# Other slots for the steps of a software pipeline, and other places for the pieces of the maxima

## The reference, cut to what matters

```python
x = x + layernorm(attn(layernorm(x)))     # first layer
x = x + layernorm(ffn(layernorm(x)))      # second layer

# attn: within one token; 16 heads of 16
Q, K, V = rms(x) @ Wq.T, ... ; pQ, pK = elu(Q), elu(K)
kv1 = sum over h of K1[h]^T V[h]; kv2 likewise with K2     # 8 x 16 each
a = Q1 @ kv1 - lmb * (Q2 @ kv2)           # per head
a = (1 - LAMBDA_INIT) * rms(a, g2); a = rms(a, g3) + a
out = gelu(a @ W1.T) @ W2.T + a

# ffn: causal attention with 16 query and 4 key heads of 16, rope,
# then a mixture of experts: 8 experts of width 512, the best 2 of each token
h = clip(x + softmax(mask(q k^T / 4)) v @ Wo)
out = clip(h + sum over the 2 experts of w * (silu(h Wg) * (h Wu)) Wd)
```

## Time and profile before

| | us |
|---|---|
| median of 3 runs | 3368.0 |
| lowest, highest | 3363.05, 3370.25 |
| the profiled execution | 3372.2 |
| its span (first to last instruction) | 3370.3 |
| mean granted clock of TensorE | 0.941 |

### The profile page before, as it was taken

One profiled execution on the slowest core, in us unless ns is written; L12 is line 12 of the kernel. 1 busy time (PEld: TensorE's weight loads), 2 busy tenths in 40 slices (PEclk: granted clock), 3 DMA queues, 4 the chain that ended last, 5 costly groups with the idle time before them and its releaser, 6 DMA issues. The chain is left out here.

```text
span 3370.3 us, 54068 instructions
## 1 busy us (share of the span) xinstructions
PE 2875.5 (85%) x17348; PEld 1707.3 (51%) x17349; DVE 2161.4 (64%) x4652; ACT 1670.3 (50%) x3836; POOL 1732.7 (51%) x2301
## 2 busy tenths in 40 slices
PE   4566899899989889989988998988759999999990
PEld 3344545554545554554555454443336666666650
DVE  3566887888898888888888888667322222222226
ACT  1234657667657656666765765765412222222224
POOL 5686746765765865776676575241212222222221
PEclk8788999999999999999999999999779999999995
DMA  1000000000000000000000000002243333333326
GB/s 46 0 10 10 11 9 14 14 25 12 27 22 14 28 20 17 22 19 23 17 22 27 12 24 19 12 25 81 73 112 53 57 58 57 58 52 58 58 43 200
DMA packets 102670, 123.21 MB, mean 37 GB/s; under 512 B 14384, under 2 KB 90160, under 8 KB 102448
## 3 DMA queue, kind: packets, MB, share of 16 engines
q1 hardware_dynamic: 76720, 85.54, 8.6%
q0 software_dynamic: 25728, 34.88, 6.0%
HBM read 58.23 MB, written 61.36 MB: 35 GB/s over the span
## 5 line engine op out<-in xcount | busy, mean ns | idle before, releaser
L822 ACT ACTIVATE wd<-SP_ 128x512 f32<-128x512 f32 (+3 forms) x1536 | 722.9, 488 | 477.9 <-PE SP_ L1439 334.0
L1105 DVE TENSOR_REDUCE NM<-MX 128x1 f32<-128x512 f32 (+3 forms) x1216 | 763.6, 655 | 243.9 <-PE MX L1396 145.2
L1393 PE MATMUL MX<-KST,QST 96*128 96x512 bf16 (+3 forms) x1536 | 457.5, 336 | 101.5 <-DVE NM L1105 89.2
L509 POOL TENSOR_TENSOR wg<-wu 128x1024 f32<-128x1024 f32 x256 | 487.4, 1924 | 106.3 <-DVE wu L941 106.2
L1436 PE MATMUL SP_<-QST,KST 99*128 99x512 bf16 (+3 forms) x1536 | 500.9, 333 | 34.3 <-ACT wd L822 15.8
L1718 POOL DMA_INDIRECT scratch_h<-Y,XG x136 | 211.2, 1553 | 604.5 <-DVE Y L1781 511.1
L1759 DVE TENSOR_TENSOR AG<-UB,SL 128x512 f32<-128x512 f32 x136 | 94.1, 692 | 460.3 <-PE UB L1798 456.9
L1736 ACT ACTIVATE SL<-GB 128x512 f32<-128x512 f32 x136 | 81.2, 597 | 603.4 <-PE GB L1798 603.4
L954 DVE TENSOR_TENSOR wg<-wu,SUM 128x1024 f32<-128x1024 f32 x256 | 310.4, 1213 | 99.7 <-PE SUM L1290 99.7
L1393 PEld LDWEIGHTS MX<-KST,QST 96*128 96x128 bf16 x1536 | 135.7, 98 | 433.9 <-DVE NM L1105 303.5
L1453 PE MATMUL OA<-wd,V 128*32 128x512 f32 (+3 forms) x3072 | 332.7, 506 | 1.0 <-ACT wd L822 0.4
(11 more groups left out here) (244 smaller groups left out, 4974.0 us busy)
## 6 DMA issues: line engine op xcount, KB each, us to landing
XG<-scratch_xs SPq DMA_DIRECT2D x136, 130.0 KB, 2.1
wu<-in_L_attn_x SPq DMA_DIRECT2D x64, 128.0 KB, 2.1
scratch_x<-wu SPq DMA_DIRECT2D x64, 128.0 KB, 1.7
scratch_h<-H SPq DMA_DIRECT2D x64, 128.0 KB, 1.7
X<-scratch_x SPq DMA_DIRECT2D x16, 512.0 KB, 4.0
HH<-scratch_h SPq DMA_DIRECT2D x16, 512.0 KB, 4.8
out<-X SPq DMA_DIRECT2D x16, 512.0 KB, 3.2
wg<-in_L_ffn_Wg SPq DMA_DIRECT2D x8, 512.0 KB
```

The lines of the kernel that those rows point to most:

```text
L509: sg["prod1"].by(pool.tensor_tensor(P1[:, k // 2, (k % 2) * hh * D:(k % 2 + 1) * hh * D].rearrange("p (h e d) -> p h e d", h=hh, e=HD), QK ...
L822: sg["exp"].by(act.activation(PR[:, n % 8, q0:512], SP_[:, n % 2, q0:512], ACT.Exp))
L1105: sg["mx"].by(dve.tensor_reduce(NM[:, u % 2, part, i, h:h + heads], MX[:, index % 2, 0:heads * n].rearrange("p (h n) -> p h n", n=n), AX.X ...
L1393: m = pe.matmul(out[:, k], QST[0:MROW, j % 2, g * G + h + k, i * P:(i + 1) * P], KST[0:MROW, keys % RK, g, 0:n], start=k == 0, stop=not la ...
```

## The change

No instruction is added or removed; steps get another slot, or another place within one. By engine:

- SP: the load of x tile p + 3 goes from slot 4 to slot 21 (tiles 0 to 2 are loaded ahead of the loop, as before); the h2 store from slot 14 (tile p - 17) to slot 0 of the next period (tile p - 18); the x1 store from slot 19 to 20.
- POOL: a period's order was `head_roots`, `gain2`, `row_root`, `copies`, `rotate`, `add_gains`, scatter 0, three `key_products`, scatter 1, `clip`, `flat_root`, `x_coefficients`, `out_coefficients`, the fourth `key_products`, scatter 2, `x1_coefficients`, scatter 3. Now it is `head_roots`, scatter 3 of the period before, `row_root`, `gain2`, `copies`, scatter 0, `rotate`, `add_gains`, three `key_products`, `clip`, `flat_root`, scatter 1, `x_coefficients`, `out_coefficients`, the fourth `key_products`, scatter 2, `x1_coefficients`.
- ACT: `squares(p - 1)` ahead of `first_part(p - 8)` in slot 2; `k_stacked` slot 12 to 14; `row_squares` slot 14 to 13; `squares2` slot 16 to 15.
- DVE: `query_products(p, 1)` from slot 7 to the head of slot 6; `add_attention` ahead of `flatten` in slot 18; `logits` slot 21 to 20.
- PE: `stack_keys` slot 12 to 13; `route` ahead of `transpose_attention` in slot 20.
- `LATE` and `AHEAD` of the maxima for rows with even j (index 0), and `share`, `LAST_BACK` and the scatters written in another way.

```diff
-        LATE, AHEAD, DONE, SPREAD = (2.5, 1.6), (9.2, 6.2), (2.0, 3.0), (3.5, 8.5)
+        LATE, AHEAD, DONE, SPREAD = (2.2, 1.6), (7.9, 6.2), (2.0, 3.0), (3.5, 8.5)
...
+        PHASE = 12 * SLOTS + 0
         LAST_PERIOD = TT + 24
-        LAST_BACK = TT + 12
+        LAST_BACK = START // SLOTS + TT
...
-            n = 32 if p % 8 < 4 else 16
-            return (i + 1) * n // SLOTS - i * n // SLOTS
+            k = p * SLOTS + i - PHASE
+            n = 16 if k < 0 or k // (NT // 2 * SLOTS) % 2 == 0 else 32
+            k %= SLOTS
+            return (k + 1) * n // SLOTS - k * n // SLOTS
...
+                        if i == 21 and have(p + 3):
+                            load(p + 3)
...
-                        if i == 4 and p >= 0 and have(p + 3):
-                            load(p + 3)
...
+                def spread(k, n):
+                    t = CH * (k // CH) + 2 * (k % CH) + n // 2
+                    scatter(t, n % 2)
...
-                        if i == 2 and have(p - 1):
+                        if i == 1 and have(p - 1):
                             head_roots(p - 1)
-                        if i == 4 and have(p - 1):
+                        if i == 2 and (p - 24) % CH < 2 and have(p - 24):
+                            spread(p - 24, 3)
+                        if i == 3 and have(p - 2):
+                            row_root(p - 2)
+                        if i == 6 and have(p - 1):
                             gain2(p - 1)
-                        if i == 4 and have(p - 2):
-                            row_root(p - 2)
...
-                        if i in (9, 12, 19, 21) and (p - 23) % CH < 2 and have(first):
-                            n = (9, 12, 19, 21).index(i)
-                            scatter(first + n // 2, n % 2)
...
                         if i == 6 and have(p):
+                            query_products(p, 1)
+                        if i == 6 and have(p):
                             query_sums(p, 0)
                         if i == 6 and have(p - 1):
                             norm_heads(p - 1)
-                        if i == 7 and have(p):
-                            query_products(p, 1)
...
+                        if i == 18 and have(p - 6):
+                            add_attention(p - 6)
                         if i == 18 and have(p - 17):
                             flatten(p - 17)
-                        if i == 18 and have(p - 6):
-                            add_attention(p - 6)
...
-                        if i == 21 and have(p - 18):
+                        if i == 20 and have(p - 18):
                             logits(p - 18)
```

More of the change, by code:

```diff
@@ L367, in load @@
                 def load(t):
+                    if t in first_loads:
+                        return
                     if t >= RX:
@@ L409, in _ @@
                     for i in range(SLOTS):
+                        if i == 0 and have(p - 18):
+                            t = p - 18
+                            need("h2", t + 1)
+                            sg["h2out%d" % (t % 2)].by(sp.dma_start(h2d[:, t, :], H2[:, t % 2]), 16)
+                        if i == 20 and have(p - 6):
+                            t = p - 6
+                            need("x1", t + 1)
+                            sp.dma_start(x1d[:, t, :], X[:, t % RX]).then_inc(stored[t % RX], 16)
+                        if i == 21 and have(p + 3):
+                            load(p + 3)
                         if p - TT in (8, 9, 10, 11) and i in (3, 15):
@@ L623, in _ @@
                             clip(p - 17)
+                        if i == 15 and (p - 23) % CH < 2 and have(p - 23):
+                            spread(p - 23, 1)
                         if i == 15 and have(p - 17):
@@ L631, in _ @@
                             key_products(p + 1, 3)
+                        if i == 20 and (p - 23) % CH < 2 and have(p - 23):
+                            spread(p - 23, 2)
                         if i == 20 and have(p - 6):
                             x1_coefficients(p - 6)
-                        first = CH * ((p - 23) // CH) + 2 * ((p - 23) % CH)
-                        if i in (9, 12, 19, 21) and (p - 23) % CH < 2 and have(first):
-                            n = (9, 12, 19, 21).index(i)
-                            scatter(first + n // 2, n % 2)
                 for r in range(2 * CH):
@@ L833, in _ @@
                             flat_turned(p - 18)
+                        if i == 2 and have(p - 1):
+                            squares(p - 1)
                         if i == 2 and have(p - 8):
                             first_part(p - 8)
-                        if i == 2 and have(p - 1):
-                            squares(p - 1)
                         if i == 2 and have(p - 7):
@@ L857, in _ @@
                             values(p + 1)
-                        if i == 12 and have(p - 8):
-                            k_stacked(p - 8)
                         if i == 13 and have(p - 17):
                             context_turned(p - 17)
-                        if i == 14 and have(p - 1):
+                        if i == 13 and have(p - 1):
                             row_squares(p - 1)
-                        if i == 16 and have(p - 17):
+                        if i == 14 and have(p - 8):
+                            k_stacked(p - 8)
+                        if i == 15 and have(p - 17):
                             squares2(p - 17)
@@ L1492, in _ @@
                             transpose_context(p - 17)
-                        if i == 12 and have(p - 8):
+                        if i == 13 and have(p - 8):
                             stack_keys(p - 8)
@@ L1502, in _ @@
                             stack_queries(p - 8, 1)
+                        if i == 20 and have(p - 18):
+                            route(p - 18)
                         if i == 20 and have(p - 2):
                             transpose_attention(p - 2)
-                        if i == 20 and have(p - 18):
-                            route(p - 18)
                         if i == 20 and have(p + 2):
```

6 lines of the change are left out of this document (5 added, 1 removed).

## The result

| | before | after |
|---|---|---|
| median | 3366.8 (5 runs) | 3381.9 (5 runs, 3378.7 to 3387.2) |
| ratio to before | | 1.0047, 95% interval 1.0032 to 1.0062 |
| profiled execution, its span | 3372.2, 3370.3 | 3380.5, 3378.6 |
| mean granted clock in that span | 0.941 | 0.937 |

The changed kernel is slower, by 15 us, where the forecast was 13 us faster. In its listing, lines from `attention()` on stand 15 further down (norm_heads L975 is L990, the maximum L1105 is L1120), POOL's 7. The page's part 1 answers the earlier trace rows: the same instructions, VectorE 3.5 and TensorE 3.8 us busier.

A forecast was written before the change was run, and what follows sets the result against it. TensorE and VectorE, both nearly full, take turns as the bound, coupled by MX's two buffers and SUM. -9 - 3 - 3 + 4 - 2 = -13 us gives 3359 profiled, 3355 as median; range 3336 to 3374.

The forecast's parts named there:

- Step 2: POOL: row_root ahead of gain2, scatter 3 behind head_roots; norm_heads keeps cover and its company on POOL: 0, bounds ±0.34 each.
- step 3: VectorE and TensorE: add_attention ahead of flatten, route ahead of transpose_attention; shortens nine long copies in routing steps: -3 us.
- Step 1: VectorE: query_products ahead of query_sums and norm_heads fills gaps before the products in long periods: -9 us, bounds -13.7 and 0.
- Steps 3 and 4: add_attention ahead of flatten, route ahead of transpose_attention, -3 us; logits to slot 20, removing TensorE's waits for it, -3 us.
- Step 5: New LATE and AHEAD: the first piece of an even row's maxima moves out of TensorE's free time: +4 us, bounds 0, +4.
- Steps 6 and 7: POOL's scatters and clip, ScalarE's moves, stack_keys, and SP's loads and stores: 0, save -2 us at the front's end.
- The tail's -2: POOL at the front's very end: one scatter moves behind clip, with add_attention's edit in the last periods: -2 us, bounds 0, -3.
- norm_heads is held up by rotate: Rival, VectorE beside POOL: each norm_heads in long and some light periods grows by 0.34 us: +6 to +8, 3362; chance 0.10.
- VectorE holds MX too long: Rival: three VectorE operations in a row without a maximum make TensorE wait: +11 to +18 us, 3379 at nearer end; chance 0.15.
- The likeliest case: The forecast itself, for the whole kernel: -13 us, to a median of 3355 us; chance 0.42.

The follow-up runs named there:

- a_old_pool_late: The changed kernel with POOL's order and LATE and AHEAD of the kernel before, other edits kept: 3359.8 us, ratio 0.9977 to the kernel before.
- b_34_products: The kernel before with query_products ahead of query_sums and norm_heads, add_attention ahead of flatten, route ahead of transpose_attention, logits in slot 20: 3358.3 us, ratio 0.9975.
- a_products_back: The changed kernel with query_products(p, 1) back behind query_sums and norm_heads on VectorE: 3374.6 us, ratio 1.0025 to the kernel before.

## Why the prediction was wrong

- **Step 2, the step that failed.** It named the case (norm_heads beside rotate), costed it at 0 and bounded it by the difference of two durations, 0.75 and 0.41 us: 0.34 in each. The runs show 1.6 to 2.1 us in each of ten hits, set by the length of the row (2.50 with four multiplications, 4.38 with eight), and TensorE's lower clock on top. The difference was misread: both durations had company already. In period 32 of the kernel before norm_heads starts 0.48 us into rotate's row and goes at once, and POOL gives way; in 33 it starts 0.54 us into it, not beside copies, and goes after the running instruction:

```profile
990.74 0.80 POOL L572 TENSOR_TENSOR RB<-Q,rope 128x160 f32<-128x160 f32 x1
...
1031.39 0.70 POOL L571 TENSOR_TENSOR RA<-Q,rope 128x160 f32<-128x160 f32 x1
```

38 of the 64 norm_heads start inside rotate's row in the kernel before, and none is held to its end; that it could be was not in the rows. A larger price was: the copy of 1.83 us, which stands still for a whole instruction of POOL, was used in step 3 and not here. The moves of scatters 0 and 3 weren't weighed for norm_heads beyond its wait for gain2, and they make the loss: with both back the time is 3354.7. For that wait the cover was read in p = 33 alone; in light periods such as 29 and 37 it was 0.1 us. The changed kernel shows no such wait, as costed, since norm_heads is later too.
- **Step 1** held: -9 forecast, -8.3 measured, and in p = 33 no gap stands between norm_heads and the next maximum. It shortens TensorE's waits for maxima by 11.5 us. VectorE in period 33 of the changed kernel answers the earlier trace rows:

```profile
1032.86 0.65 DVE L990 TENSOR_TENSOR wu<-wu,R 128x256 f32<-128x256 f32 x1
1033.42 1.14 DVE L1120 TENSOR_REDUCE NM<-MX 128x1 f32<-128x512 f32 x2
```

- **Steps 3 and 4**, -3 and -3: the waits changed as told. But five of the 16 copies were long (1.83 us), not nine; four took 0.40 to 0.62 and seven 0.16 or 0.17, so step 3 was too large from its own rows. The copy of 1.83 us is 1.57 now and TensorE's wait behind it 0.83 instead of 1.09, below; the sums of period 37 have no wait. The time did not follow.
- **Step 5**, +4: wrong in sign, -3 to -7. Perhaps the pieces that come one or two slots later help more than the first one costs; no run shows where the gain comes from.
- **Steps 6 and 7**, ScalarE, SP and `stack_keys` 0: right as far as can be told (a_old_pool_late less b_34_products is +1.5, within the intervals). The tail's -2 did not come: from the start of period 63 to that of the last `clip` both kernels take 393.8 us.
- **TensorE's clock** was not in the sum. It makes half of the difference in the long stretch.

```profile
1092.21 1.57 DVE L1073 CAST FX<-topi 128x4 f32<-128x4 uint32 x1
```

```profile
1095.85 1.97 PE L1296 MATMUL SUM<-ident,wg 128*128 128x128 f32 x16 [0.83 <-DVE BR L1098]
```

The rivals: "norm_heads is held up by rotate" was the right mechanism with a price five to six times too small; "VectorE holds MX too long" had the right sign and the wrong mechanism. The likeliest case, 3355, is near what the kernel takes once POOL's order is left alone (3352.4), but in part by luck: the -6 of steps 3 and 4 isn't seen, and the +4 of step 5 turned into a gain.

## What to carry to other kernels

Before a step is moved on GpSimd or on VectorE, list for each VectorE operation with two SBUF inputs what GpSimd has back to back around its start; bound a meeting by the whole row, not by one instruction, above all with an indirect DMA of GpSimd shortly ahead, and see whether two edits, harmless alone, bring such a pair together. Where an instruction's duration varies by a multiple in a trace, look at the other engine of that moment before taking the mean. A stall that leaves TensorE idle is to be priced with the lower clock behind it.

## What was not expected of the hardware

- The hold of norm_heads: it takes up to 0.94 us when it is let in after the running instruction, 1.25 to 2.51 us (4.39 with the longer row) when it isn't, from starts that look alike to 0.01 us (0.64 and 2.28 above). A scatter shortly ahead seems to be part of the condition. In the 17 traces 586 norm_heads start inside the row, a scatter directly ahead of it counted in. For 101 of them a scatter had begun less than 5 us earlier, and 42 of these were held; for the other 485 the last scatter was over 8 us back, or none had come yet, and none was held, though in 317 of these POOL stood idle for less than 0.12 us ahead of the row. This is a correlation; what decides among the 101 isn't settled, and no edit took the scatters away by themselves. The Trainium skill ("SBUF — State Buffer", section "Who interferes with whom") has the one that issues first keep the ports that both share for the whole instruction while the other fully blocks; the trace agrees that a waiting VectorE instruction blocks fully, but in the 42 holds it stayed blocked through up to four and eight instructions, not through one.
- The clock: after the hold TensorE was granted 0.50 while it worked without a gap. Stretches at the lower level come without a hold too, and one kernel's runs spread by 26 us with them (a_products_back, 3366.4 to 3392.1, the clock 0.937 to 0.928). Why they come in one run and not in the next is open; it limits what such a comparison can tell to some 3 to 6 us, the half widths of the intervals above with 8 to 12 runs.
